# Scaling rows of q and k by their norms on GpSimd: two instructions of four heads in place of one of eight

## The chip, the cores and the metric

The kernel runs on one core of a Trainium2 chip. The metric is the device time of one execution in microseconds. Engines are named as the profile names them: PE is TensorE (PEld its weight loads), DVE is VectorE, ACT is ScalarE, POOL is GpSimd, SP is SyncE.

## The reference

A layer normalisation of x (8 batches of 256 tokens, 128 wide), and on its result an attention and a mixture of experts, both added to x. Cut to the part that matters here:

```python
q = (xn @ Wq).reshape(b, n, h, dh)            # 16 heads of 64
k, v = split(x @ Wkv)
k = concat([null_k, k]); v = concat([null_v, v])   # two null keys a head
q = q / max(norm(q), 1e-12) * q_scale
k = k / max(norm(k), 1e-12) * k_scale
sim = q @ k.T * 8 + slopes * -abs(j - i); causal mask
out = softmax(sim) @ v  -> @ Wout
x = x + out + shared_expert(xn) + routed_top2_of_8_experts(xn)
```

The norm of each token's q and k is taken head by head: 64 numbers, one reciprocal norm.

## The kernel before

Every engine has its own hand-written program; semaphores tie them together. After the set-up (weights split into high and low parts, routing, tokens scattered by expert) come the expert matmuls over 39 tiles, and then the attention, batch by batch, 256 tokens each. A batch has 16 steps, one for each head, software-pipelined: at step s DVE takes the row maxima of head s (L887), ACT exponentiates head s-1 (L663), DVE divides head s-2 by its sum in two instructions, one of 128x130 and one of 128x258 (both L902; called the first and the second multiply below), PE transposes head s-3 (L1095), and later come the product with v (L1085, L1086) and with Wout (L1118).

Beside the heads run side jobs, set by the table `JOBS` (what happens at which step, and in which of two PSUM banks). A job "kq" projects 512 columns (8 heads) of q or k for one tile of 128 tokens of the next batch: three PE matmuls (L958 to L960), ACT squares and copies (L601, L602), DVE sums the squares of each head (L871) and clips them (L875), POOL raises them to the power -0.5 (L428 for k, L431 and L434 for q) and multiplies the 128x512 rows by them in place (L444, in `scale_by_norm`). A batch has eight such jobs, at steps 1, 4, 5, 6, 7, 11, 12 and 13; POOL's part comes one step later. A job "tr" transposes the scaled rows on PE (L1053), which waits for the semaphore `kqn` of L444.

POOL works in the order of its program. In a step it does the norms and the scaling of the job, then, in odd steps, copies the null keys' probabilities of the last two heads to `pnull` (L479, two small copies, after the wait for both L902 multiplies), and at step 6 it copies slots and weights (L488, L489) and issues four indirect DMAs that gather the experts' results (L493). ACT's exponential of head h waits, beside the row maxima, for the L479 copies of the pair of heads that used the same `prob` buffer six heads before.

Of the kernel before, what the change touches and what calls it, by code (L numbers as in the profile page):

```python
# [10 lines left out]
ALU = mybir.AluOpType  # L11
# [6 lines left out]
HEADS, DH, NNULL = 16, 64, 2  # L18
# [22 lines left out]
def build(nc, a, out):  # L41


    with ExitStack() as ctx:
        def sb(name, shape, dt=F32):
            return ctx.enter_context(nc.sbuf_tensor(name, shape, dt))
# [97 lines left out]
        ssm, rpow, rnorm = (sb(n, [P, 8, HEADS // 2]) for n in ("ssm", "rpow", "rnorm"))  # L144
# [62 lines left out]
        g = type("Sems", (), S)  # L207
# [7 lines left out]
        def bc(ap, n):  # L215

            return ap.unsqueeze(2).to_broadcast([ap.shape[0], ap.shape[1], n])
# [70 lines left out]
        def nth(c, w, t):  # L288

            return 4 * c + 2 * (1 - w) + t  # L290
# [73 lines left out]
        def _(pool):  # L364
            gp = nc.gpsimd
# [71 lines left out]
            def scale_by_norm(b, job):  # L437
                kind, c, w, t, i, n = job
                if kind == "kq":
                    j = nth(c, w, t)  # L440
                    pool.wait_ge(g.r_ready, 8 * (b + 1) + j + 1)
                    pool.wait_ge(left[i], n + 1)
                    rows = (qtok if w else ktok)[t][:, c * 512:(c + 1) * 512].rearrange("p (h d) -> p h d", d=DH)
                    gp.tensor_tensor(rows, rows, bc(rnorm[:, j, :], DH), ALU.mult).then_inc(g.kqn, 1)  # L444

            def split_for_queries(n):
                xs, cols = xs2[n % 2], bass.ds(n * SEQ, SEQ)
# [4 lines left out]
            def entry(part, b, steps=range(HEADS)):  # L452
                whose = PARTS[part]
                nb = b + 1
                for s in steps:
# [11 lines left out]
                    for _, job_b, job in (behind(part, b, s, 1) if part != "ahead" else []):  # L467
                        norms(job_b, job)
                        scale_by_norm(job_b, job)
# [32 lines left out]
            for s in range(AHEAD):  # L502
                for _, job_b, job in behind("ahead", -1, s, 1):
                    norms(job_b, job)
                    scale_by_norm(job_b, job)
# [703 lines left out]
```

## Time and profile before

| | us |
|---|---|
| median of 3 runs (lowest, highest) | 478.66 (478.4, 479.74) |
| the profiled execution, its own time | 479.73 |
| its span, first to last instruction | 478.0 |
| busy: PE, DVE, ACT, POOL | 421.6, 366.7, 357.9, 294.3 |
| granted TensorE clock, mean over the span | 0.961 |

The span is what the profiler saw between the first and the last instruction; about 1.7 us lie around it. One batch of the attention takes 40.7 us.

### The profile page before, as it was taken

What the parts mean: (1) busy time and instruction counts of PE and PEld (TensorE: products, weight loads), DVE (VectorE), ACT (ScalarE), POOL (GpSimd) and SP (SyncE); (2) the same over time, 40 slices, a digit from 0 to 9 for tenths busy, and PEclk for the clock granted to TensorE, in tenths of its full rate; (3) what the DMA queues carried; (4) which work ended last, traced back from release to release, by engine and by line L of the source; (5) the groups of instructions that cost most, each with busy time, mean ns of one, the idle gap of its engine ahead of it and who ended that gap; (6) DMA issues with size and microseconds to landing.
All of it is one profiled execution on the core that took longest, in us unless ns stands there. A gap on an engine that the chain in (4) does not pass through costs nothing.

```text
span 478.0 us, 10590 instructions
## 1 busy us (share of the span) xinstructions
PE 421.6 (88%) x2793; PEld 305.1 (64%) x2793; DVE 366.7 (77%) x1419; ACT 357.9 (75%) x1097; POOL 294.3 (62%) x444
## 2 busy tenths in 40 slices
PE   3846805999998899999999999999999999999995
PEld 3734503667776676676666776776676677767663
DVE  5699602666652898899799889989988997997884
ACT  3344702666665979988997998899799899989874
POOL 3748779910001589579768848966875894785400
PEclk9969855999999999999999999999999999999998
DMA  8971112222221000000001001000100100010000
GB/s 234 319 247 34 56 49 60 62 73 81 77 73 39 1 25 0 2 24 23 3 1 45 2 1 47 0 2 2 44 2 2 45 2 2 14 32 2 24 23 12
DMA packets 29738, 21.36 MB, mean 45 GB/s; under 512 B 3528, under 2 KB 27376, under 8 KB 29552
## 3 DMA queue, kind: packets, MB, share of 16 engines
q1 hardware_dynamic: 26816, 16.46, 11.7%
q0 software_dynamic: 2048, 4.20, 2.9%
q8 instruction: 25, 0.41, 0.4%
q14 instruction: 33, 0.27, 0.2%
q10 hardware_dynamic: 816, 0.03, 0.1%
HBM read 12.41 MB, written 8.26 MB: 43 GB/s over the span
## 4 chain that ended last, share of the span: by engine, by line
PE 54%; DVE 18%; issue 9%; ACT 8%; POOL 7%; DMA 3%; ACTq 1%; DVEq 0%
POOL slot_x L418 7%; PE bank L1104 7%; PE bank L1095 7%; PE bank L958 6%; PE bank L959 5%; PE bank L960 5%; DVE arena_b L887 4%; PE bank L1053 4%; PE bank L1085 4%; PE bank L1172 4%; PE bank L1118 4%; DVE arena_b L902 3%; DMA arena_b<-slot_x 2%; DVE probT L912 2%; DVE ssq L871 2%
## 5 line engine op out<-in xcount | busy, mean ns | idle before, releaser
L663 ACT ACTIVATE arena_b<-arena_b,nmx 128x130 f32<-128x130 f32 (+1 forms) x256 | 114.9, 458 | 16.3 <-PE bank L1095 8.3
L887 DVE CUSTOM_DVE_ANT_0 arena_b<-bank,bias 128x130 f32<-128x130 f32 (+1 forms) x256 | 81.2, 355 | 29.8 <-PE bank L1104 15.7
L902 DVE TENSOR_SCALAR arena_b<-arena_b,rden 128x130 f32<-128x130 f32 (+1 forms) x256 | 84.9, 375 | 4.5
L431 POOL TENSOR_TENSOR rpow<-ssm,mhalf 128x8 f32<-128x8 f32 x32 | 52.5, 1641 | 45.3 <-DVE ssm L875 45.3
L444 POOL TENSOR_TENSOR arena_b<-arena_b,rnorm 128x512 f32<-128x512 f32 x64 | 66.9, 1045 | 5.1 <-POOL rnorm L434 0.2
L1095 PE MATMUL bank<-ident,arena_b 128*128 128x128 f32 x384 | 67.0, 283 | 2.4 <-DVE arena_b L902 2.3
L1104 PE MATMUL bank<-arena_a 64*128 64x130 f32 (+1 forms) x512 | 59.5, 351 | 0.8 <-ACT arena_a L624 0.8
L1095 PEld LDWEIGHTS bank<-ident,arena_b 128*128 128x128 f32 x384 | 44.1, 141 | 22.0 <-DVE arena_b L902 13.1
L428 POOL TENSOR_TENSOR rnorm<-ssm,mhalf 128x8 f32<-128x8 f32 x32 | 52.7, 1646 | 0.9
L663 ACT ACTIVATION_READ_ACCUMULATOR arena_b<-arena_b,nmx 128x1 f32 x256 | 51.2, 200 | 0.0
L871 DVE TENSOR_REDUCE ssq<-arena_b 128x8 f32<-128x512 f32 x64 | 43.6, 682 | 4.7 <-ACT arena_b L601 3.9
L1085 PE MATMUL bank<-probT,arena_a 128*64 128x256 f32 x256 | 42.4, 404 | 1.8 <-DVE probT L912 0.8
L418 POOL DMA_INDIRECT slot_x<-arena_a,slot x32 | 34.3, 1071 | 15.6 <-issue 9.3
L601 ACT ACTIVATE arena_b<-bank 128x512 f32<-128x512 f32 x64 | 38.5, 602 | 6.2 <-PE bank L960 4.6
L479 POOL COPY pnull<-arena_b 128x4 f32<-128x4 f32 x128 | 22.3, 207 | 32.5 <-DVE arena_b L902 32.5
L1053 PE MATMUL bank<-ident,arena_b 128*128 128x128 f32 x256 | 39.6, 278 | 2.9 <-ACT arena_a L614 1.1
L1104 PEld LDWEIGHTS bank<-arena_a 64*128 64x128 f32 x512 | 33.6, 186 | 12.4 <-issue 8.9
L912 DVE COPY probT<-bank 128x384 f32<-128x384 f32 x64 | 35.4, 553 | 5.1 <-DVE arena_b L841 2.1
L1053 PEld LDWEIGHTS bank<-ident,arena_b 128*128 128x128 f32 x256 | 29.3, 140 | 14.7 <-issue 3.6
L602 ACT ACTIVATE arena_b<-bank 128x512 f32<-128x512 f32 x64 | 38.5, 602 | 0.0
L1118 PE MATMUL bank<-oT,wo 128*128 128x256 f32 x128 | 38.2, 381 | 0.0
L651 ACT ACTIVATE probT<-bank 128x384 f32<-128x384 f32 x64 | 31.8, 496 | 5.8 <-PE bank L1095 5.7
(196 smaller groups left out, 969.4 us busy)
## 6 DMA issues: line engine op xcount, KB each, us to landing
slot_x<-probT SPq DMA_DIRECT2D x3, 832.0 KB, 8.6
arena_b<-slot_x SPq DMA_DIRECT2D x39, 64.0 KB, 1.9
slot_y<-arena_b SPq DMA_DIRECT2D x39, 64.0 KB, 1.5
arena_a<-in_L_attn_x_dram SPq DMA_DIRECT2D x2, 512.0 KB, 5.3
arena_b<-in_L_ffn_wd_dram SPq DMA_DIRECT2D x1, 1024.0 KB, 9.9
arena_b<-in_L_attn_Wkv_dram SPq DMA_DIRECT2D x1, 1024.0 KB, 8.8
arena_b<-in_L_attn_x_dram SPq DMA_DIRECT2D x8, 128.0 KB, 2.6
out_dram<-arena_b SPq DMA_DIRECT2D x8, 128.0 KB, 2.0
```

The source lines that it names most:

```text
L418: pool.indirect_dma_start(xg_dram, bass.IndirectOffsetOnAxis(ap=slot[:, n // TOPK, n % TOPK:n % TOPK + 1], axis=0), xn1[:, n // TOPK, :], ...
L428: gp.tensor_tensor(rnorm[:, j, :], ssm[:, j, :], mhalf[:, 0:HEADS // 2], ALU.pow).then_inc(g.r_ready, 1)
L444: gp.tensor_tensor(rows, rows, bc(rnorm[:, j, :], DH), ALU.mult).then_inc(g.kqn, 1)
L663: sc.activation(prob[:, (HEADS * b + h) % RP, c], sim[h % 2][:, c], ACT.Exp, scale=-1.0, bias=nmx[:, h % HEADS, t:t + 1], accum_out=den[:, ...
L871: ve.reduce_sum(ssq[j % 2][:], sqb[j % 2].rearrange("p (h d) -> p h d", d=DH), AX.X).then_inc(g.red, 1)
L887: ve.tensor_tensor_reduce(out=sim[h % 2][:, c], in0=bank[h % 2][:, c], in1=bias[:, c], scale=-SLOPES[h], scalar=3e38, op0=ALU.add, op1=ALU ...
L902: ve.tensor_scalar(pr, pr, rden[:, h % HEADS, t:t + 1], None, ALU.mult).then_inc(g.pn, 1)
L1053: ins = te.transpose(side[i][:, q * P:(q + 1) * P], src[:, p * P:(p + 1) * P], ident[:])
L1085: te.matmul(opair[r, 0:SEQ], v[:, 0, hh * DH:(hh + 1) * DH], probT[half][:, 0:SEQ], start=True, stop=False)
L1095: ins = te.transpose(bank[2 + h % 2][:, k * P:(k + 1) * P], prob[:, (HEADS * b + h) % RP, c:c + P], ident[:])
L1104: ins = te.matmul(bank[half][:, c0:c1], qT[r, h // 2, q0:q0 + P], kT[r, h // 2, 0:c1 - c0], start=True, stop=True)
L1118: te.matmul(bank[6][:, 0:SEQ], wo[:, p % PAIRS, :], oT[p % 2][:], start=p == 0, stop=p == -1).then_inc(g.oread, 1)
```

## The change

The one 128x512 multiply of L444 becomes two of 128x256, four heads each. The semaphore is raised by the second. Nothing else is changed; later lines move down by two (L479 is L481 in the changed kernel, L902 is L904).

```diff
                     rows = (qtok if w else ktok)[t][:, c * 512:(c + 1) * 512].rearrange("p (h d) -> p h d", d=DH)
-                    gp.tensor_tensor(rows, rows, bc(rnorm[:, j, :], DH), ALU.mult).then_inc(g.kqn, 1)
+                    for r in (slice(0, 4), slice(4, 8)):
+                        ins = gp.tensor_tensor(rows[:, r, :], rows[:, r, :], bc(rnorm[:, j, r], DH), ALU.mult)
+                    ins.then_inc(g.kqn, 1)
```

POOL's program from step 5 to step 8 of a batch, before (`arena_b` holds qtok, ktok and the probabilities):

```order
L431 TENSOR_TENSOR rpow<-ssm,mhalf 128x8
L434 TENSOR_TENSOR rnorm<-rpow,rslope 128x8
L444 TENSOR_TENSOR arena_b<-arena_b,rnorm 128x512
L479 COPY pnull<-arena_b 128x4 x2
L428 TENSOR_TENSOR rnorm<-ssm,mhalf 128x8
L444 TENSOR_TENSOR arena_b<-arena_b,rnorm 128x512
L488 COPY slot_now<-slot 128x4
L489 COPY w_now<-wts 128x4
L493 DMA yg_odd<-slot_y,slot_now 128x128 x4
L428 TENSOR_TENSOR rnorm<-ssm,mhalf 128x8
L444 TENSOR_TENSOR arena_b<-arena_b,rnorm 128x512
L479 COPY pnull<-arena_b 128x4 x2
```

The same place of POOL's program in the changed kernel:

```order
L431 TENSOR_TENSOR rpow<-ssm,mhalf 128x8
L434 TENSOR_TENSOR rnorm<-rpow,rslope 128x8
L445 TENSOR_TENSOR arena_b<-arena_b,rnorm 128x256 x2
L481 COPY pnull<-arena_b 128x4 x2
L428 TENSOR_TENSOR rnorm<-ssm,mhalf 128x8
L445 TENSOR_TENSOR arena_b<-arena_b,rnorm 128x256 x2
L490 COPY slot_now<-slot 128x4
L491 COPY w_now<-wts 128x4
L495 DMA yg_odd<-slot_y,slot_now 128x128 x4
L428 TENSOR_TENSOR rnorm<-ssm,mhalf 128x8
L445 TENSOR_TENSOR arena_b<-arena_b,rnorm 128x256 x2
L481 COPY pnull<-arena_b 128x4 x2
```

Each of the 64 scalings is now a pair, nothing stands between its two halves, and all else keeps its place; the programs of the other engines are the same.

## Rows read from the trace of the kernel before

**Rows 1.** The page: engines, busy us, share of the span, instructions.

```profile
PE 421.6 (88%) x2793; PEld 305.1 (64%) x2793; DVE 366.7 (77%) x1419; ACT 357.9 (75%) x1097; POOL 294.3 (62%) x444
```

**Rows 2.** The page: the chain that ended last, by engine.

```profile
PE 54%; DVE 18%; issue 9%; ACT 8%; POOL 7%; DMA 3%; ACTq 1%; DVEq 0%
```

**Rows 3.** Chain in order of time, 331 to 343 us: start, us, what.

```profile
337.31 0.14 issue
337.44 0.35 DVE arena_b L902
...
340.08 0.88 issue
340.96 0.35 DVE arena_b L902
341.31 0.04 issue
341.36 0.55 PE bank L1095 x3
```

**Rows 4.** Timeline of DVE, 331 to 343 us.

```profile
332.57 0.22 DVE L875 TENSOR_SCALAR ssm<-ssq 128x8 f32<-128x8 f32 x1
...
337.24 0.55 DVE L902 TENSOR_SCALAR arena_b<-arena_b,rden 128x130 f32<-128x130 f32 x2
...
340.02 1.28 DVE L902 TENSOR_SCALAR arena_b<-arena_b,rden 128x130 f32<-128x130 f32 x2
```

**Rows 5.** Timeline of POOL, 285 to 365 us.

```profile
306.86 1.04 POOL L444 TENSOR_TENSOR arena_b<-arena_b,rnorm 128x512 f32<-128x512 f32 x1
...
328.75 1.04 POOL L444 TENSOR_TENSOR arena_b<-arena_b,rnorm 128x512 f32<-128x512 f32 x1
...
331.71 1.04 POOL L444 TENSOR_TENSOR arena_b<-arena_b,rnorm 128x512 f32<-128x512 f32 x1
...
339.91 1.04 POOL L444 TENSOR_TENSOR arena_b<-arena_b,rnorm 128x512 f32<-128x512 f32 x1
340.90 0.45 POOL L479 COPY pnull<-arena_b 128x4 f32<-128x4 f32 x2
```

**Rows 6.** Timeline of DVE, 305 to 318 us.

```profile
307.30 0.63 DVE L875 TENSOR_SCALAR ssm<-ssq 128x8 f32<-128x8 f32 x1
...
309.68 0.17 DVE L875 TENSOR_SCALAR ssm<-ssq 128x8 f32<-128x8 f32 x1
```

**Rows 7.** POOL's groups: line, shapes, count, busy us, mean ns, idle before.

```profile
L444 POOL TENSOR_TENSOR arena_b<-arena_b,rnorm 128x512 f32<-128x512 f32 x64 | 66.9, 1045 | 5.1 <-POOL rnorm L434 0.2
...
L465 POOL TENSOR_TENSOR arena_r<-xn1T,arena_r 128x256 fp32r<-128x256 f32 x7 | 5.1, 731 | 0.6
...
L400 POOL TENSOR_TENSOR arena_a<-arena_a,rstd 128x1024 f32<-128x1024 f32 x1 | 1.9, 1895 | 0.1
...
L403 POOL TENSOR_TENSOR vsum<-nmean 128x16 f32<-128x16 f32 x1 | 0.2, 214 | 1.8 <-DVE nmean L752 1.8
```

**Rows 8.** Timeline of PE, 339.5 to 350 us.

```profile
347.81 0.60 PE L1053 MATMUL bank<-ident,arena_b 128*128 128x128 f32 x4
```

**Rows 9.** Busy time of each engine from 341.3 to 372 us.

```profile
341.30:372.00 30.70, 30.50 (x215) 22.02 (x215) 26.88 (x112) 28.21 (x88) 22.45 (x36) 1.00 0.01 2
```

**Rows 10.** Timeline of ACT, 331 to 343 us.

```profile
341.97 0.41 ACT L663 ACTIVATE arena_b<-arena_b,nmx 128x130 f32<-128x130 f32 x1 [1.42 <-PE bank L1095]
```

**Rows 11.** First batch of the attention: timeline of POOL, 160 to 190 us.

```profile
177.55 1.11 POOL L444 TENSOR_TENSOR arena_b<-arena_b,rnorm 128x512 f32<-128x512 f32 x1
178.61 0.37 POOL L479 COPY pnull<-arena_b 128x4 f32<-128x4 f32 x2
```

**Rows 12.** First batch: timeline of DVE, 166 to 182 us.

```profile
177.28 0.08 DVE L887 DVE_READ_ACCUMULATOR2_ANT nmx<- 128x1 f32 x1
...
177.47 1.34 DVE L902 TENSOR_SCALAR arena_b<-arena_b,rden 128x130 f32<-128x130 f32 x2
```

**Rows 13.** First batch: timeline of ACT, 176 to 181 us.

```profile
179.07 0.41 ACT L663 ACTIVATE arena_b<-arena_b,nmx 128x130 f32<-128x130 f32 x1 [2.27 <-DVE nmx L887]
```

## The prediction

> **What bounds the kernel now.** I read first the page's engine totals [rows 1]: PE is busy 88% of the span, POOL 62%. Then the chain that ended last [rows 2]: PE 54%, DVE 18%, and 9% "issue", time in which an engine waited for nothing that the profile shows. POOL's 7% lies in the scatter before the experts, ahead of the first scaling. So POOL's own speed looks harmless, and I looked for whoever waits for it. The direct customer of the scaled rows, PE's transposes L1053, is far away: the scaling that starts at 339.91 ends at 340.95 [rows 5] and its transposes start at 347.81 [rows 8], 6.9 us later. No likely lengthening of a scaling reaches that far.
>
> The chain in order of time shows something else. An ordinary pair of L902 multiplies has an "issue" of 0.14 us between its parts (337.31), but once in a batch this is 0.88 us (340.08) [rows 3]; on DVE's timeline the ordinary pair takes 0.55 us (337.24) and that one 1.28 (340.02) [rows 4]. What is special at 340.02 is that POOL began L444 at 339.91 [rows 5]. In the same way L875 takes 0.17 us alone and 0.63 when it starts at 307.30, inside the L444 that starts at 306.86 [rows 5, 6]. So a DVE instruction that meets L444 is held. From when to when: the first multiply of the held pair did its work (1.28 - 0.55 = 0.73) late, at 340.75, which is 0.84 after L444's start; L875 really started at 307.30 + 0.46 = 307.76, 0.90 after. The second multiply starts 0.20 behind the first (337.24 to 337.44 [rows 3, 4]), in the held pair at 340.96. L444 is thus let go 0.20 us before its recorded end, and 0.15 before the next POOL instruction starts (339.91 to 340.90 [rows 5] is 0.99). The Trainium skill ("SBUF — State Buffer", section "Who interferes with whom") has a rule for it: GpSimd and a DVE operation in a two-port mode take a shared port pair in turns, whoever comes first holds it for the whole instruction, and the other blocks. By that rule the trace agrees on who blocks, but here the hold ends 0.2 us before the recorded end; it comes back among the rivals.
>
> What bounds a batch around this place: from about 331 to 341.3 us DVE works back to back and the chain runs on DVE; the second multiply at 340.96 releases PE at 341.36 [rows 3], and from there PE is busy 30.50 of 30.70 us [rows 9], until DVE's stretch of the next batch. So what moves that one second multiply moves the batch. Other meetings of L444 with DVE in the PE-bound stretch cost nothing as they stand, and gain nothing when shortened.
>
> **The price of a half.** No row has a 128x256 multiply by a broadcast norm. The line through 16, 512 and 1024 columns (214, 1045 and 1895 ns [rows 7]) has 1.66 ns a column: 1045 - 256 x 1.66 = 620 ns. The bound below is half of 1045, 522 ns, as if an instruction cost nothing by itself; the bound above is L465, 731 ns, a 128x256 with two full inputs [rows 7]. I take 620, as three rows lie on its line. The next instruction starts about 0.055 us before a recorded end (340.95 against 340.90 [rows 5]), so the second half starts 0.565 after the first, and a pair keeps POOL 1.13 us where it was 0.99: 0.14 more. Busy time of POOL grows by 64 x 0.195 = 12.5 us, to about 307. Eight of the 64 pairs lie ahead of the experts' end, and POOL stands idle behind them until the experts are done: nothing.
>
> **What a half does to DVE.** Each half holds the port from its start to 0.42 (620 less 0.2), and between 0.42 and 0.565 it is free. That a DVE instruction gets in there is shown by the rows: the held multiply ran at 340.75, before the L479 at 340.90 [rows 4, 5], which waited for nothing. But behind the first multiply comes the second, 0.20 later, and the second half comes between them: it takes the port at 0.565 and holds the second multiply until 0.565 + 0.42 = 0.985. Such a case is in the trace: in the first batch L444 started at 177.55, 0.08 after the first multiply, and the pair took 1.34 [rows 11, 12], all of it by the second multiply.
>
> **The sum, one batch.** L444 at 328.75, then 331.71, then 339.91 [rows 5]: POOL works without a pause from the first to the last of these, so the last starts 2 x 0.14 = 0.28 later, at 340.19. Meanwhile L875 at 332.57 [rows 4] meets the second half of the scaling before it (start 331.85, second half to 332.84) and is held to the end of it, 0.22 later than now (it starts its work at 332.62 now, 0.05 of its 0.22 being held time against 0.17). DVE has no pause behind it, so the first multiply arrives at 340.24, 0.05 behind L444's start, waits to 340.61, and the second waits to 340.19 + 0.985 = 341.17, where it started at 340.96: 0.21 later. In short the batch pays 3 x 0.14 - 0.20; a hold of DVE that came earlier has no say in it. There are six such batches: 6 x 0.21 = +1.3 us.
>
> **The first batch** differs. ACT's exponential at 179.07 [rows 13] had its row maxima at 177.36 [rows 12]; it really waited for the L479 copies that end at 178.98 [rows 11]. The two pairs ahead of them and their own add 3 x 0.14, less the 0.07 by which L444 was itself late there and what DVE took of the copies: about +0.25. The last batch has no scalings. Elsewhere POOL's lateness is hidden: copies against exponentials have 0.62 us in the other batches (341.35 to 341.97 [rows 5, 10]), and need 3 x 0.14.
>
> Sum: 1.3 + 0.25 = 1.5 us. Against the profiled execution's own time, 479.73, that is 481.2; that execution was 1.07 above the median of the three runs. On the median 478.66 it is 480.2; I round to 480.1, since a PE that is late has now and then a gap to make it up. The least that a measurement of this kernel can tell is about 0.3%, 1.4 us, so this lies on the edge.
>
> **Rivals.**
> - *The multiply slips ahead of the scaling.* The margin is 0.05 us. If POOL is later by more than that, the first multiply runs at once and the second is held only by the first half, to 0.08 + 0.42 behind: 340.67, 0.29 earlier than now. But then the copies at about 341.8 hold the exponential of 341.97, which cannot gain more than some 0.2. Six times -0.2 to -0.3, and +0.25: 477.1 to 477.8, and the faster end if all batches do it. For it: the margin; against it: it takes away at most 0.3. Chance 0.15. This is the rival on the other side; it decides from a POOL lateness of about 0.33 us.
> - *The port is not let go between halves of one kind.* Then the first multiply waits to 0.985 and the second to 1.185: 0.41 a batch later, 6 x 0.41 + 0.25 = +2.7, 481.4. For it: two halves with nothing between; against it: L479 follows L444 just as closely, and DVE gets in. Chance 0.13. The Trainium skill's rule in the section named above, taken to the letter (the port is held for the whole instruction), gives this case: a recorded half of 0.62 us would still hold when the next starts at 0.565.
> - *A half costs what L465 costs*, 731 ns. A pair then adds 0.36, the last scaling is 0.72 late, and the copies 1.08: the exponential at 341.97 waits 0.46 longer, and +1.0 in the first batch: 6 x 0.46 + 1.0 = +3.8, 482.4. The Trainium skill ("GPSIMD Engine Reference", section 3.1) gives about 2.6 cycles at 1.2 GHz for an element of a two-input tensor_tensor; with the 195 ns of the line's foot that would be an estimate of 750 ns, the side of L465. Against it stand L444 and L400 themselves, at 1.66 ns. Chance 0.08.
> - *It is hidden after all*: DVE or PE makes up the 0.2 in a gap. 478.7 to 479.3. Chance 0.14.
> - The forecast, 479.3 to 481.0: chance 0.50, a little over half of it within 0.3%.
>
> **How the numbers follow.** Faster by over 0.3% (below 477.2): 0.09 of the first rival. Slower (above 480.1): 0.23 of the forecast, 0.13 and 0.08: 0.44. Within: the remaining 0.27 of the forecast, 0.06 and 0.14: 0.47. The range goes from the lower end of the first rival with both bounds of a half, 476.8, to the third, 482.2.
>
> **What would show it.** POOL: 128 instructions of 128x256 at about 620 ns, the second 0.565 behind the first. DVE: the pair of multiplies at the same place of each batch still near 1.3 us, with a first part of about 0.65 and a second part held too; L875 ahead of it with a hold of 0.2 to 0.3 where it had 0.05. The start of PE's L1095 there 0.2 later within a batch; a batch of 40.9 us in place of 40.7. Copies L481 must still end before the exponential in all batches but the first. I am wrong if the held second multiply is gone, if halves last over 0.68 us, or if the exponential waits for copies in every batch.

## The result and the profile after

The changed kernel takes 480.52 us (median of 19 runs, 479.16 to 483.42), the kernel before 478.66 us (median of 19 runs on the same chip, 477.62 to 481.26). The ratio is 1.0045, 95% interval 1.0029 to 1.0060: slower by 2.1 us (1.4 to 2.9); the two medians lie 1.9 us apart. The forecast was 480.1 us in a range of 476.8 to 482.2, with chances of 0.44 for slower, 0.47 for no difference and 0.09 for faster.

The page of the changed kernel: engines, and the groups of POOL that matter (line, shapes, count, busy us, mean ns, idle before).

```profile
PE 423.1 (88%) x2793; PEld 305.4 (64%) x2793; DVE 366.1 (76%) x1419; ACT 358.2 (75%) x1097; POOL 301.8 (63%) x508
...
L445 POOL TENSOR_TENSOR arena_b<-arena_b,rnorm 128x256 f32<-128x256 f32 x128 | 75.8, 613 | 5.1 <-POOL rnorm L434 0.2
```

A half takes 613 ns where 620 were forecast. POOL's total grew by 7.5 us where 12.5 were forecast. The forecast added up whole records, but the records of two halves overlap: the 128 of them cover 75.8 us and not 128 x 0.613 = 78.5, and the copies to `pnull` take 1.5 less. POOL's timeline in the batch of [rows 5]:

```profile
328.94 1.18 POOL L445 TENSOR_TENSOR arena_b<-arena_b,rnorm 128x256 f32<-128x256 f32 x2
330.07 0.31 POOL L481 COPY pnull<-arena_b 128x4 f32<-128x4 f32 x2
330.33 1.63 POOL L428 TENSOR_TENSOR rnorm<-ssm,mhalf 128x8 f32<-128x8 f32 x1
332.04 1.18 POOL L445 TENSOR_TENSOR arena_b<-arena_b,rnorm 128x256 f32<-128x256 f32 x2
...
340.37 1.18 POOL L445 TENSOR_TENSOR arena_b<-arena_b,rnorm 128x256 f32<-128x256 f32 x2
341.50 0.38 POOL L481 COPY pnull<-arena_b 128x4 f32<-128x4 f32 x2
```

From the start of a pair to the next instruction it is 1.13 us (328.94 to 330.07), where a whole scaling had 0.99: 0.14 more. From the first of these pairs to the third it is 11.43 us, where it was 11.16 [rows 5]: the 2 x 0.14 of the forecast. DVE's timeline beside it:

```profile
331.01 0.55 DVE L904 TENSOR_SCALAR arena_b<-arena_b,rden 128x130 f32<-128x130 f32 x2
...
332.75 0.50 DVE L877 TENSOR_SCALAR ssm<-ssq 128x8 f32<-128x8 f32 x1
...
340.49 1.22 DVE L904 TENSOR_SCALAR arena_b<-arena_b,rden 128x130 f32<-128x130 f32 x2
```

L877 (L875 before) takes 0.50 us where it took 0.22 [rows 4]: it meets the second half of the pair that starts at 332.04. This is what DVE loses on its own way through the batch: from the multiplies of head 4 to those of head 8 it takes 12.93 us (327.56 to 340.49), where it took 12.65 (327.37 to 340.02). The pair of multiplies takes 1.22 us where it took 1.28 [rows 4]. The chain in order of time shows where these 1.22 go now:

```profile
340.49 0.06 DVE arena_b L904
340.55 0.44 issue
340.99 0.73 DVE arena_b L904
341.72 0.04 issue
341.76 0.55 PE bank L1097 x3
```

Before there was one wait of 0.88 between the multiplies and an ordinary second one of 0.35 [rows 3]. Now the wait between them is 0.44 and the second multiply itself lasts 0.73: the first got in between the two halves, some 0.41 after the pair's start at 340.37 (340.99 less the ordinary 0.20 from the first to the second), and the second, which does its work in the last 0.35 of its record, was held by the second half until 341.37 or so, 1.0 after that start. The forecast had 0.42 and 0.985.

For the length of a batch, ACT's exponential of head 10 is a good mark, since it runs behind the held multiplies once in each batch. In the changed kernel it starts in the second and in the seventh batch at

```profile
219.54 0.41 ACT L665 ACTIVATE arena_b<-arena_b,nmx 128x130 f32<-128x130 f32 x1 [1.27 <-PE bank L1097]
...
424.30 0.41 ACT L665 ACTIVATE arena_b<-arena_b,nmx 128x130 f32<-128x130 f32 x1 [1.35 <-PE bank L1097]
```

so a batch takes (424.30 - 219.54) / 5 = 40.95 us. In the kernel before the same two starts are 219.72 and 423.43: 40.74. The difference is 0.21 us a batch, the number of the forecast. The granted clock is 1.00 over these five batches in both traces. In the first batch the same exponential:

```profile
178.66 0.40 ACT L665 ACTIVATE arena_b<-arena_b,nmx 128x130 f32<-128x130 f32 x1 [2.72 <-POOL pnull L481]
```

The profile now names the copies as what it waited for. Counted from the first transposes of the attention (147.99 before, 147.13 after) it starts 31.53 us in, where it was 31.08: 0.45 later. From these transposes to the end it is 330.00 us before and 331.73 after. The profiled executions themselves differ by less (spans 478.0 and 478.9), as that of the changed kernel came to the attention 0.86 us sooner. The eight scalings before it are no reason for that: POOL waits for the experts behind them, 50.7 us here. The granted clock of the first 147 us was 0.93 here and 0.88 before; that this is the reason was not tried.

### The profile page after: what moved, and what is told of

Same layout as the page of the kernel before. It is cut to its first block, busy times and chain, and to the rows that moved or that the text cites. A ratio compares the mean times of both kernels' runs of the same rounds, so it can differ in the third digit from the quotient of the medians.

```text
span 478.9 us, 10654 instructions
## 1 busy us (share of the span) xinstructions
PE 423.1 (88%) x2793; PEld 305.4 (64%) x2793; DVE 366.1 (76%) x1419; ACT 358.2 (75%) x1097; POOL 301.8 (63%) x508
## 4 chain that ended last, share of the span: by engine, by line
PE 54%; DVE 17%; POOL 10%; issue 8%; ACT 6%; DMA 2%; ACTq 1%; DVEq 0%; SPq 0%; POOLq 0%
POOL slot_x L418 7%; PE bank L1106 7%; PE bank L1097 7%; PE bank L960 6%; PE bank L961 5%; PE bank L962 5%; PE bank L1174 4%; PE bank L1087 4%; PE bank L1055 4%; DVE arena_b L889 4%; PE bank L1120 4%; DVE arena_b L904 3%; DVE probT L914 2%; PE bank L1155 2%; DVE arena_b L866 2%
## 5 line engine op out<-in xcount | busy, mean ns | idle before, releaser
L904 DVE TENSOR_SCALAR arena_b<-arena_b,rden 128x130 f32<-128x130 f32 (+1 forms) x256 | 85.8, 378 | 4.5
L431 POOL TENSOR_TENSOR rpow<-ssm,mhalf 128x8 f32<-128x8 f32 x32 | 52.5, 1640 | 43.6 <-DVE ssm L877 43.5
L445 POOL TENSOR_TENSOR arena_b<-arena_b,rnorm 128x256 f32<-128x256 f32 x128 | 75.8, 613 | 5.1 <-POOL rnorm L434 0.2
L428 POOL TENSOR_TENSOR rnorm<-ssm,mhalf 128x8 f32<-128x8 f32 x32 | 52.7, 1648 | 0.2
L481 POOL COPY pnull<-arena_b 128x4 f32<-128x4 f32 x128 | 20.8, 195 | 30.4 <-DVE arena_b L904 30.3
```

Source lines behind the costliest of these rows:

```text
L428: gp.tensor_tensor(rnorm[:, j, :], ssm[:, j, :], mhalf[:, 0:HEADS // 2], ALU.pow).then_inc(g.r_ready, 1)
L431: gp.tensor_tensor(rpow[:, j, :], ssm[:, j, :], mhalf[:, 0:HEADS // 2], ALU.pow).then_inc(g.pw, 1)
L445: ins = gp.tensor_tensor(rows[:, r, :], rows[:, r, :], bc(rnorm[:, j, r], DH), ALU.mult)
L904: ve.tensor_scalar(pr, pr, rden[:, h % HEADS, t:t + 1], None, ALU.mult).then_inc(g.pn, 1)
```

## The experiments

The first four kernels ran on another chip than the pair above, where the kernel before took 484.58 us; each ratio is against the kernel before on the same chip. The length of a batch is worked out from the same two starts as above, in the one trace that there is of each kernel; the five batches of a trace differ by at most 0.11 us, and the granted clock over them is 1.00 in every one. For the other chip there is no trace of the kernel before, so the first four lengths are set against the 40.74 of this one.

| kernel | ratio (95%) | starts of the mark | batch, us |
|---|---|---|---|
| before | 1 | 219.72, 423.43 | 40.74 |
| changed: all scalings in halves | 1.0045 (1.0029 to 1.0060) | 219.54, 424.30 | 40.95 |
| halves in step 7 only | 0.9997 (0.9971 to 1.0024) | 222.07, 425.40 | 40.67 |
| halves in steps 5 and 6 only | 1.0045 (1.0021 to 1.0069) | 223.00, 428.02 | 41.00 |
| halves in all other steps | 0.9987 (0.9965 to 1.0009) | 220.24, 423.89 | 40.73 |
| whole, copies ahead of step 7's scaling | 1.0005 (0.9981 to 1.0029) | 221.59, 426.16 | 40.91 |
| the same, and a wait for head 8 | 0.9906 (0.9884 to 0.9928) | 217.71, 419.06 | 40.27 |
| halves with copies ahead and the wait | 0.9971 (0.9952 to 0.9990) | 217.55, 420.23 | 40.54 |
| all in quarters | 1.0129 (1.0102 to 1.0155) | 223.26, 430.63 | 41.47 |
| whole, the wait, copies behind | 1.0031 (1.0009 to 1.0052) | 219.71, 424.27 | 40.91 |

**One part of the change alone.** In the first three kernels the split is kept for a part of the scalings:

```diff
+                    parts = (slice(0, 4), slice(4, 8)) if j == 3 else (slice(0, 8),)
-                    for r in (slice(0, 4), slice(4, 8)):
+                    for r in parts:
```

with `j == 3` for step 7, `j in (1, 2)` for steps 5 and 6, and `j not in (1, 2, 3)` for the rest. Step 7 alone:

> Only the scaling that POOL does in step 7 (j = 3, the one at 339.91 us in the trace of before) is split, the other seven of a batch stay whole. Theory (lateness of POOL plus the hold of the second half decide): the second multiply starts 0.985 us after the scaling's start where it was 1.05, so a batch gets 0.06 us shorter, and the first batch 0.14 longer by the later copies: -0.2 us, same as before within 0.1%. Rival (the split of this scaling is itself the cost, because its second half holds DVE's second multiply): +0.2 us a batch, +1.3 us, ratio 1.0027.

Measured: 40.67 us a batch, 0.07 less than before. The split of the very scaling that holds DVE is no cost; it even gives a little, as the sum had it (0.985 in place of 1.05). The ratio agrees with no difference, and its interval ends below the rival's 1.0027, if not by much.

> Only the scalings of steps 5 and 6 (j = 1 and 2) are split; the one of step 7 is whole. Theory: POOL comes to step 7's scaling 0.29 us later, DVE's first multiply still finds it there and is held to its 0.84, so a batch gets 0.29 us longer (0.15 if the multiply slips ahead and only the second is held): +1.7 us and +0.3 in the first batch, +2.0 us, ratio 1.004 (1.0025 to 1.0045), as much as the whole change. Rival (the step 7 split is the cost): nothing, ratio 1.000.

Measured: 41.00 us a batch, 0.26 more than before, and the ratio of the whole change. Here POOL and the chain show a whole scaling that is only late; its timeline, and then the chain:

```profile
343.94 1.04 POOL L446 TENSOR_TENSOR arena_b<-arena_b,rnorm 128x512 f32<-128x512 f32 x1
```

```profile
344.07 0.07 DVE arena_b L905
344.13 0.86 issue
344.99 0.35 DVE arena_b L905
```

The first multiply (344.07) again arrives just behind the scaling (343.94) and is held as before. What the batch pays is that both are later: POOL by its two pairs, and DVE because its L878, at 336.33, is held to 0.50 us by the second half of step 6. This kernel doesn't tell the two apart; two of those below do.

> The other five scalings of a batch (j = 0, 4, 5, 6, 7) are split, those of steps 5 to 7 whole. Theory: these lie where PE is the bound and heads have 1.5 us or more between DVE's multiplies and PE's transposes; ratio 1.000 within 0.1%, with the same 40.7 us a batch. Rival (POOL's added busy time or the added meetings with DVE cost everywhere): five eighths of the whole, +1.3 us, ratio 1.0028.

Measured: 40.73 us a batch, ratio 0.9987 with 1 in its interval. Halves where PE is the bound cost nothing. This length and the 40.74 come from different chips and agree within 0.01 us, which speaks for comparing lengths across the two. The three parts add up by batch: -0.07 + 0.26 - 0.01 = 0.18, the whole 0.21.

**Taking the hold away, first try.** POOL's program in step 7, with whole scalings (`step` is the list of the step's jobs):

```diff
                         norms(job_b, job)
-                        scale_by_norm(job_b, job)
+                        if s != 7:
+                            scale_by_norm(job_b, job)
                     if h is not None and h % 2:
...
                                            two[:, :, c0:c0 + NNULL]).then_inc(g.pnc, 1)
+                    for _, job_b, job in step:
+                        if s == 7:
+                            scale_by_norm(job_b, job)
```

> Before's kernel with whole scalings, but in step 7 POOL first waits for DVE's multiplies and copies to pnull, and then scales the rows. Theory (the hold of DVE by step 7's scaling is on the chain once a batch): both multiplies run at once, 0.74 us earlier in each of six batches, and the scaling then meets the next head's multiplies, which have 0.8 us to spare: -3.5 to -4.4 us, ratio 0.991 to 0.993. Rival (DVE's hold was cover for PE or ACT, which bound the batch anyway): less than 1 us, ratio above 0.998.

Measured: 40.91 us a batch, 0.17 more, ratio 1.0005. The expectation was wrong, and not the theory of the hold but my reading of who runs beside whom. I had taken the copies' wait, for heads 4 and 5, to be a wait for the held multiplies. The held ones are of head 8: POOL is here three steps behind DVE. The timelines of POOL and DVE show it:

```profile
219.25 0.31 POOL L481 COPY pnull<-arena_b 128x4 f32<-128x4 f32 x2
219.53 1.03 POOL L444 TENSOR_TENSOR arena_b<-arena_b,rnorm 128x512 f32<-128x512 f32 x1
```

```profile
219.48 1.44 DVE L907 TENSOR_SCALAR arena_b<-arena_b,rden 128x130 f32<-128x130 f32 x2
```

POOL did not wait for anything; the copies only put the scaling 0.28 us later. The first multiply's record now starts 0.05 us ahead of the scaling's, and it was held all the same: alone it lasts 1.17 us where 0.29 is ordinary, and the second does its work 1.04 after the scaling's start. So this is the price of a later POOL by itself. Against DVE's multiply the scaling starts 0.16 us later than before (0.05 behind its start, where it was 0.11 ahead), no clip of DVE is held longer (L880 of step 6 takes 0.21), and PE waits 0.57 us for the second multiply where it waited 0.42: the batch's 0.17. That the ratio is still near 1 fits with the first batch: the copies that hold the exponential there come ahead of the scaling now, and the mark lies 30.45 us behind the first transposes, 0.63 sooner than before.

**Second try, with a wait for the right head.** To the kernel above is added

```diff
                         if s == 7:
+                            pool.wait_ge(g.pn, TB * (HEADS * b + 9))
                             scale_by_norm(job_b, job)
```

> Whole scalings; in step 7 POOL copies to pnull first, then waits until DVE has divided head 8 (the pair of multiplies that was held), and then scales. POOL runs about three heads behind DVE here, so this wait, unlike the one for heads 4 and 5, is a real one. Theory: the held pair of multiplies runs at once, the second 0.74 us earlier, and a batch takes 40.0 us in place of 40.74: -4.4 us in six batches, ratio 0.991 (0.989 to 0.994). Rival (PE or ACT bounds the batch as soon as the hold is gone): a batch of 40.5 us or more, ratio above 0.997.

Measured: ratio 0.9906, 475.04 us against 478.75: the best kernel of this study. The ratio is the expected one, but not for the reason expected: a batch takes 40.27 us, 0.47 less, and not 0.74 less, and the first batch gives the rest. POOL waits 0.55 us, the multiplies run at once, and PE's timeline shows where the rest stayed:

```profile
297.72 1.04 POOL L444 TENSOR_TENSOR arena_b<-arena_b,rnorm 128x512 f32<-128x512 f32 x1 [0.55 <-DVE arena_b L908]
```

```profile
297.09 0.55 DVE L908 TENSOR_SCALAR arena_b<-arena_b,rden 128x130 f32<-128x130 f32 x2
```

```profile
297.13 0.66 PE L1091 MATMUL bank<-probT,arena_a 128*64 128x256 f32 x4
297.58 0.42 PE L1092 MATMUL bank<-probT,arena_a 128*64 128x128 f32 x4
297.94 0.55 PE L1101 MATMUL bank<-ident,arena_b 128*128 128x128 f32 x3
```

The second multiply ends at 297.64, but PE is in the product with v until about 298.0. In the kernel before:

```profile
340.06 0.66 PE L1085 MATMUL bank<-probT,arena_a 128*64 128x256 f32 x4
340.51 0.42 PE L1086 MATMUL bank<-probT,arena_a 128*64 128x128 f32 x4
341.36 0.55 PE L1095 MATMUL bank<-ident,arena_b 128*128 128x128 f32 x3 [0.42 <-DVE arena_b L902]
```

From the start of the product to that of the transposes it was 1.30 us and is 0.81: 0.49 less. PE had stood idle 0.42 of it, and about that is all that an earlier multiply could give. Over the whole attention this trace gains 3.9 us: 1.20 in the first batch (the mark lies 29.88 us behind the first transposes, where it was 31.08), 3.0 in the six steps from mark to mark that follow, and it loses 0.25 in the last batch.

> The changed kernel (all scalings in halves) with the same wait in step 7. Theory: the batch no longer pays for POOL's lateness in step 7, but L875 in front of it is still held by the second half of step 6's scaling, 0.2 to 0.3 us: a batch of 40.2 to 40.3 us, ratio to before 0.993 (0.991 to 0.996), slower than the same wait with whole scalings by 0.002 to 0.004. Rival (halves cost by POOL's time alone): the same as with whole scalings.

Measured: 40.54 us a batch, 0.27 more than with whole scalings, ratio 0.9971. It had been expected at 40.2 to 40.3, with a ratio of 0.991 to 0.996, because the 40.0 under it was too low; the difference of a batch, 0.2 to 0.3, was as expected. The ratios differ by 0.0065, where 0.002 to 0.004 were expected; 0.43 us of that lie in the first batch (30.31 against 29.88). POOL waits for DVE at step 7 here, so its own lateness is out of it, and the hold of L875 by the second half of step 6's scaling costs by itself: it is 0.51 us long in this trace (L883 there), behind the pair that starts at 288.96:

```profile
289.66 0.51 DVE L883 TENSOR_SCALAR ssm<-ssq 128x8 f32<-128x8 f32 x1
```

```profile
288.96 1.19 POOL L445 TENSOR_TENSOR arena_b<-arena_b,rnorm 128x256 f32<-128x256 f32 x2
```

**More of the same.** Each scaling in four:

```diff
-                    for r in (slice(0, 4), slice(4, 8)):
+                    for r in (slice(2 * k, 2 * k + 2) for k in range(4)):
```

> Before's order, every scaling in four instructions of two heads. By the line of POOL's prices one takes 0.40 us and holds 0.2, a scaling keeps POOL about 1.38 us, 0.4 more than whole. Step 7's scaling starts 0.8 us late, after DVE's pair of multiplies, which then runs at once (0.74 us earlier, less up to 0.2 by L875's hold), but the copies end 1.2 us late and hold the exponential of head 10, by 0.6 us. Theory A (that exponential then leads the batch): a batch of 41.1 to 41.4 us, ratio 1.005 to 1.009. Theory B (only the second multiply leads it): a batch of 40.0 to 40.3, ratio 0.991 to 0.995.

Measured: 41.47 us a batch, ratio 1.0129; theory A holds, and its size was too low: the batch is 0.07 above its range, and the ratio 0.004 above, as the first batch alone adds 1.6 us, which had been left out. A quarter takes 404 ns (forecast 400), four of them 1.48 us to the next instruction where 1.38 were forecast. ACT's exponential of head 10 waits for the copies in every batch; its row beside POOL's:

```profile
304.36 1.53 POOL L445 TENSOR_TENSOR arena_b<-arena_b,rnorm 128x128 f32<-128x128 f32 x4
305.84 0.31 POOL L481 COPY pnull<-arena_b 128x4 f32<-128x4 f32 x2
```

```profile
306.23 0.40 ACT L665 ACTIVATE arena_b<-arena_b,nmx 128x130 f32<-128x130 f32 x1 [2.00 <-DVE nmx L889]
```

The profile names DVE's maxima, but these were ready at about 304.8 in this trace; the copies end at 306.15, 0.08 ahead of the exponential. It is the case in which the releaser that is named had long been done.

**The wait, with the copies behind the scaling**, as they stand in the kernel before:

```diff
                         norms(job_b, job)
+                        if s == 7:
+                            pool.wait_ge(g.pn, TB * (HEADS * b + 9))
                         scale_by_norm(job_b, job)
```

> Whole scalings, the wait for head 8 in step 7 as above, but with the copies to pnull behind the scaling, as before. The multiplies run 0.74 us earlier, and the copies end at 341.9 by the clock of before's trace where they ended at 341.35, so the exponential of head 10 starts at about 342.0, as before. Theory A (that exponential leads the batch once the hold is gone): a batch near 40.7 us, ratio 0.999 to 1.001. Theory B (only the second multiply leads it): 40.0 us, ratio 0.991.

Measured: 40.91 us a batch and a ratio of 1.0031, near A and 0.1 us a batch over its upper end. The multiplies run free here too, and all of their gain is lost to the exponential, which starts 0.07 us after the copies' end:

```profile
301.10 0.45 POOL L481 COPY pnull<-arena_b 128x4 f32<-128x4 f32 x2
```

```profile
301.62 0.40 ACT L665 ACTIVATE arena_b<-arena_b,nmx 128x130 f32<-128x130 f32 x1 [1.62 <-POOL pnull L481]
```

## Why the prediction was right

- *The price of a half*: 613 ns against 620; a pair keeps POOL 0.14 us longer, as forecast. The rival at 731 ns fell.
- *DVE gets in between the halves*: the first multiply did, 0.41 us after the pair's start. The rival in which halves of one kind don't let go fell.
- *The second multiply meets the second half*: its record of 0.73 us shows it.
- *The batch pays for the two scalings ahead*: 0.21 us measured against 0.21; split in parts, 0.26 for the two scalings ahead, -0.07 for the one that holds, nothing for the rest.
- *"A hold of DVE that came earlier has no say in it"*: this was wrong, though the sum does not show it. POOL came to step 7 later by 0.27 us, and DVE by 0.28, because the second half of step 6 held L877; each has a price by itself. A POOL that is 0.16 later against DVE costs 0.17 a batch (copies ahead of the scaling), and the longer hold costs 0.27 where POOL waits for DVE (halves with the wait). Here the two run side by side and are paid once. Had DVE not been held there, its multiply would have come at 340.21 by these numbers, 0.16 ahead of the scaling: the rival below.
- *The multiply slips ahead*: it did not. The margin was 0.12 us (340.37 to 340.49) where I had 0.05, since L875 was held 0.28 longer where I had 0.22. Even without that, 0.05 ahead would not have been enough: in the kernel with the copies ahead the multiply starts so and is held, while 0.08 ahead, in the first batch of the kernel before [rows 11, 12], it was not.
- *The first batch*: that the copies hold the exponential was right, the size was not. I put its delay at about 0.25 us, 3 x 0.14 less some relief, and it was 0.45. The relief was there: from the start of the third scaling to the copies' end it is 1.44 us where it was 1.43, so the 0.14 of this pair cost nothing, and the two pairs ahead of it gave 0.31. What I missed is a fourth pair, that of step 2. It makes POOL's L452 (L450 before, a part of splitting tokens into high and low) 0.15 later, this holds DVE's multiplies beside it longer (0.87 us for 0.77), and POOL gets the clipped sums for its next job 0.14 later:

```profile
161.09 0.73 POOL L452 TENSOR_TENSOR arena_r<-xn2T,arena_r 128x256 fp32r<-128x256 f32 x1
163.62 1.65 POOL L431 TENSOR_TENSOR rpow<-ssm,mhalf 128x8 f32<-128x8 f32 x1 [1.79 <-DVE ssm L877]
```

```profile
161.31 0.87 DVE L904 TENSOR_SCALAR arena_b<-arena_b,rden 128x130 f32<-128x130 f32 x2
```

This L431 starts 16.49 us behind the first transposes, where it started 16.35 behind them (164.34) before. In the kernel with halves in all other steps that pair is the only one ahead of the mark, and the mark lies 31.19 us in, 0.11 later than before.
- *The sum*: 6 x 0.21 + 0.25 = 1.5 us forecast; the trace has 1.73 from the first transposes of the attention to the end, the two medians differ by 1.9, and the ratio makes 2.1 (1.4 to 2.9). What is left between trace and ratio, 0.4, is unexplained and within the interval.
- *That it is hidden in PE's gaps*: it was not; the batch's 0.21 arrived whole. I rounded down for this, and was wrong to. The chances leaned the same way, with a little more for no difference (0.47) than for slower (0.44).
- *The range*: its upper end was said to be the third rival's time, which is 482.4 by its own sum and not 482.2. It does not bear on the result.
- What the prediction did not see: the wait of 0.88 that it turned on was worth no more than about the 0.42 us for which PE stood idle before the transposes. For a delay that is no matter; for a gain, as in the kernel with the right wait (0.47), it is the bound.

## What to carry to other kernels

An engine with 62% busy time and no waiting customer can still set the time, if its instructions hold up another engine's: look for the same instruction with two durations, and for what began just before the long one. When an instruction is cut in pieces, count its extra time into the start of everything behind it on that engine, and ask which of these later starts meets something on the chain; here it was harmless to split the scaling that holds, and not to split the two ahead of it. Ask too where the later pieces hold the other engine longer than before. Where two engines collide once a batch on the chain, one wait for the right item on the one that has slack, with what others need put in front of it, can take the collision away: here it gave 0.94%, about twice what the cutting cost. Neither half of it does so alone, the copies ahead (ratio 1.0005) or the wait (1.0031).

## What the runs showed that I had not expected

Not every instruction of POOL holds DVE. The raising to a power takes 1.63 us on POOL, longer than any scaling, and does not hold DVE: in the changed kernel L428 starts at 330.33, and the pair of multiplies at 331.01 takes its ordinary 0.55 us (both rows above). In the attention of the kernel before, 50 first multiplies start inside such a raising, and none takes more than 0.293 us; 20 start inside a scaling, and they take 0.55 to 1.02. Nor is every instruction of DVE held: its sums of squares (L871) take 0.68 us and its row maxima (L887) 0.29 inside a scaling as outside. A quarter of 0.40 us can be met without loss as well: multiplies that start 0.19 to 0.28 us behind its start take 0.29 to 0.34, those that start up to 0.06 behind it 0.42 to 0.48. The raising works on 8 columns and a scaling on 128 or more, so whether the operation or the size makes the difference was not tried.
